# Eight matmuls of a shared network moved from ahead of the first slot table to behind the third

## The reference, cut to what matters

```
scores = softmax(flat_x @ gate_w.T).T
topk_weight, topk_idx = top_k(scores, C)          # C = 148 tokens for each of 16 experts
xg = flat_x[topk_idx]
h  = gelu(xg @ Wg.T) * (xg @ Wu.T)                 # per expert, 1024 wide
eo = (h @ Wd.T) * topk_weight
out = scatter_add(eo) + (gelu(x @ Sg.T) * (x @ Su.T)) @ Sd.T   # shared network, 512 wide
```

## Time and profile before

| | |
|---|---|
| runs shown | 535.07, 536.86, 537.45 us |
| median | 536.86 us |
| profiled execution | 538.24 us, span 536.4 us |
| TensorE matmul | 470.9 us busy (88%) |
| VectorE | 395.4 us (74%) |
| ScalarE | 228.5 us (43%) |
| GpSimd | 192.2 us (36%) |
| mean granted clock of TensorE | 0.957 |
| HBM read, written | 63.32 MB, 5.33 MB |

### The profile page before, as it was taken

How to read it: one execution, slowest core, us unless ns; L and a number is a source line. 1 busy time by engine, 2 the same in 40 slices (tenths; PEclk the granted TensorE clock), 3 DMA queues, 4 the chain that set the end, 5 groups by cost and what they waited for, 6 DMA issues and landing times.

```text
span 536.4 us, 10728 instructions
## 1 busy us (share of the span) xinstructions
PE 470.9 (88%) x3873; PEld 409.7 (76%) x3873; DVE 395.4 (74%) x694; ACT 228.5 (43%) x529; POOL 192.2 (36%) x252
## 2 busy tenths in 40 slices
PE   6968989889898986969998886999999999999990
PEld 3546867759577683959786675889999999999990
DVE  1398998989989898696227969768866777667730
ACT  1413463544545446121334300455556665566610
POOL 1313245363543634040210005128444453454242
PEclk9989999999999999788987999899999999999996
DMA  7855110100000000000000000697888898899521
GB/s 243 334 201 222 34 41 1 42 10 31 23 18 10 10 0 10 1 10 1 10 11 6 1 2 21 214 384 265 282 292 315 319 324 294 298 331 328 174 26 12
DMA packets 17344, 69.05 MB, mean 129 GB/s; under 512 B 4338, under 2 KB 10399, under 8 KB 12834
## 3 DMA queue, kind: packets, MB, share of 16 engines
q1 hardware_dynamic: 12130, 61.96, 31.0%
q0 software_dynamic: 4608, 5.41, 4.9%
q10 hardware_dynamic: 576, 1.29, 0.7%
HBM read 63.32 MB, written 5.33 MB: 128 GB/s over the span
## 4 chain that ended last, share of the span: by engine, by line
PE 62%; DVE 13%; POOL 6%; ACT 6%; issue 5%; DMA 3%; DVEq 0%; POOLq 0%; SPq 0%; ACTq 0%
PE bank L1446 16%; PE bank L1457 11%; PE bank L1231 7%; PE bank L1204 7%; PE bank L1217 6%; POOL tmp L423 3%; PE bank L1355 3%; PE bank L1243 3%; DMA wex_s<-in_wex 2%; DVE scratch L994 2%; PE bank L1158 2%; DVE wproj_s L977 2%; ACT L539 2%; PE bank L1193 1%; POOL rstd L425 1%
## 5 line engine op out<-in xcount | busy, mean ns | idle before, releaser
L423 POOL TENSOR_SCALAR tmp<-mv 128x1 f32<-128x1 f32 x30 | 34.0, 1134 | 164.7 <-DVE mv L792 164.7
L507 POOL DMA_INDIRECT out_rows<-scratch,slot_s x32 | 52.1, 1629 | 85.4 <-DMA out_rows<-scratch,slot_s 66.0
L1457 PE MATMUL bank<-scratch,wex_s 128*128 128x148 f32 x512 | 77.7, 295 | 0.5 <-DVE scratch L1086 0.5
L1457 PEld LDWEIGHTS bank<-scratch,wex_s 128*128 128x128 f32 x512 | 67.6, 190 | 1.0 <-DVE scratch L1086 1.0
L496 POOL DMA_INDIRECT xg<-token_rows,slot_g x32 | 40.1, 1253 | 75.2 <-issue 59.8
L736 ACT ACTIVATE scratch<-bank 128x296 f32<-128x296 f32 x64 | 26.6, 416 | 69.5 <-PE bank L1446 69.5
L1446 PE MATMUL bank<-scratch,wfc_s 128*128 128x148 f16 x512 | 52.8, 228 | 0.8 <-DVE wproj_s L977 0.8
L1446 PE MATMUL bank<-scratch,wsh_s 128*128 128x148 f16 x512 | 52.7, 227 | 0.0
L1446 PE MATMUL bank<-scratch,wproj_s 128*128 128x148 f16 x256 | 50.7, 227 | 0.0
L1086 DVE SCALAR_TENSOR_TENSOR scratch<-bank,scratch 128x296 f32<-128x296 f32 x64 | 29.5, 461 | 27.1 <-ACT scratch L736 26.9
L977 DVE SCALAR_TENSOR_TENSOR wproj_s<-wex_s,wfc_s 128x512 f16<-128x512 f32 x64 | 40.4, 683 | 11.2 <-ACT wfc_s L719 11.2
(11 more groups left out here) (164 smaller groups left out, 943.6 us busy)
## 6 DMA issues: line engine op xcount, KB each, us to landing
wex_s<-in_wex SPq DMA_DIRECT2D x16, 2048.0 KB
wex_s<-in_wex SPq DMA_DIRECT2D x16, 1024.0 KB, 8.5
patch_s<-in_patches SPq DMA_DIRECT2D x10, 384.0 KB
token_rows<-y_s SPq DMA_DIRECT2D x10, 128.0 KB, 1.7
out_rows<-h_all SPq DMA_DIRECT2D x5, 256.0 KB
wfc_s<-in_wfc SPq DMA_DIRECT2D x1, 1024.0 KB, 5.1
wproj_s<-in_wproj SPq DMA_DIRECT2D x1, 1024.0 KB, 7.3
wsh_s<-in_wsh SPq DMA_DIRECT2D x1, 1024.0 KB, 9.0
```

The lines of the kernel that those rows point to most:

```text
L423: gp.tensor_scalar(tmp[:, k:k + 1], var, EPS, None, ALU.add).then_inc(p_chain, 1)
L507: gp.indirect_dma_start(out, bass.IndirectOffsetOnAxis(slot_s[b][:], 0), eo[b], None, compute_op=ALU.add).then_inc(scattered, 16)
L1457: last = pe.matmul(ps_down[k][:, 0:C], wex_s[s.par][:, lo:lo + P], hexT[:, m, :], start=(m == 0), stop=(m == MC - 1))
```

## The change

After the thresholds are found and the prefix sums made, 30 matmuls of the shared network's down projection remain. Before, 18 of them stand ahead of the first slot table, 4 behind it, 4 behind the second, none behind the third, and 4 behind the transposes of the first expert's rows. After, 10 stand ahead of the first table and 8 behind the third one. Their order among themselves is the same.

```diff
             left = STEPS + 4 * TILES - BEFORE - sum(BESIDE)
-            assert left >= 12
-            fill(left - 12)
+            assert left >= 20
+            fill(left - 20)
             pe.wait_ge(digits_made, 1)
             slots(0)
             fill(4)
             slots(1)
             fill(4)
             slots(2)
+            fill(8)
```

## The result

| | before | after |
|---|---|---|
| runs | 6: 535.05 to 537.45 us | 6: 532.09 to 533.78 us |
| median | 536.50 us | 532.83 us |
| profiled execution, span | 538.24, 536.4 us | 532.39, 530.6 us |
| mean granted clock | 0.957 | 0.969 |

The changed kernel is faster: ratio 0.9937, 95% interval 0.9916 to 0.9958, that is 3.4 us (2.3 to 4.5). Values from 0.9943 to 0.9958, that is 2.3 to 3.1 us, fit both measurements. Three of the 64 runs of the kernel before in the later comparisons took 695 to 1650 us and are left out of the ratios.

What follows compares the result with a forecast made beforehand. TensorE was taken as the bound, VectorE leading from 325.4 to 335.0 us. 0.9 us from the earlier table and 2.2 from the clock made 3.1 off 538.24, giving 535.1; the median lies 1.4 lower, so 533.8, range 532.4 to 537.0.

Steps and rivals of the forecast that it cites:

- (a): Ahead of the first slot table: with eight matmuls fewer, VectorE takes that table 0.9 us earlier.
- (b): VectorE's run from first to third table: keeps its 9.46 us, as each piece still finds its input.
- (c): Behind the third table: the moved matmuls' 3.50 us fit in the 3.79 us stall, costing nothing at full clock.
- (d): Transposes to first expert's products: full clock kept, products 3.1 us earlier together with (a), 2.2 of it the clock's.
- (e): Downstream, third expert's weights: the last shared tile releases their queue earlier too, so idle time stays; term 0.
- Rival 1: Gap ahead of the first table: the clock falls there instead; gain 0.9 us (536.0) or 2.6 (534.3); chance 0.15.
- rival 2: From the gap ahead of the first table: the clock falls and does not recover; slower, 539.2 us; chance 0.08.
- Rival 3: Expert stage: third expert's weights set the pace and the lead is lost; 536.0 us; chance 0.15 together with Rival 4.
- Rival 4: Only (a) is gained, the clock falling elsewhere ahead of the experts; 535.9 us; chance 0.15 together with Rival 3.
- rival 2's full case: The extreme of rival 2, the clock falling ahead of the first table without recovering: 540.5 us.
- The rule weighed: TensorE's clock: avoid idle gaps above about 3 us; the new 1.9 us gap would be harmless, giving 533.8 us.

Runs made afterwards that it cites:

- e3: The change with twelve matmuls moved behind the third slot table instead of eight; ratio to the kernel before 1.0034.
- e1: The kernel before with 16 unused matmuls between the third slot table and the wait ahead of the transposes, nothing moved; ratio 0.9967.
- e6: The change with 14 unused matmuls (3.0 us) between the last shared tile and the first expert; ratio to the kernel before 0.9957.
- e7: The change with SyncE waiting for two pairs of the first expert's products before issuing the second expert's down weights; ratio to the kernel before 1.0023.
- e11: The changed kernel itself, measured and profiled again beside three others; ratio to the kernel before 0.9957.
- e4: The change with the eight matmuls put behind the transposes of the first expert's rows instead of ahead of them; ratio to the kernel before 1.0064.
- e8: The change with SyncE issuing the third expert's gate and up weights ahead of its wait for the shared tiles; ratio to the kernel before 0.9900.
- e10: e8 with five unused matmuls ahead of the first search round; ratio to the kernel before 0.9884.
- e9: The kernel before with SyncE issuing the third expert's gate and up weights ahead of its wait for the shared tiles; ratio 0.9950.
- e2: The change with four matmuls moved behind the third slot table instead of eight; ratio to the kernel before 0.9953.

## Why the prediction was right, and where it was not

The time came out at 532.83, forecast 533.8, range 532.4 to 537.0; forecast 3.1 us less, measured 3.4 and, again, 2.3. The first products of the third expert are 2.5 us earlier; the profiles do not show where the rest of the 3.4 comes from.

(a) **Right.** VectorE takes the first table 0.99 us earlier (forecast 0.9), and TensorE waits 1.80 us for the one-hot (forecast 1.9).

(b) **Right.** VectorE's run is 9.44 us long (forecast 9.46). None of the sums came late, though two tiles fewer are done at the first table.

(c) **Right.** The moved eight fit, and 0.23 us of waiting are left (forecast 0.3). e3 shows the bound: with four more TensorE is the late one.

(d) **Right in its size, not in its path.** The first products are 2.99 us earlier (forecast 3.1), and e1 shows 2.0 of them to be the clock's (forecast 2.2). But the low half of the rows, which was to be late next, was done 1.74 us after the transposes' start (333.27, forecast 2.02), and the products began at 2.25 us, when the four matmuls behind the transposes ended (333.86 in the chain).

(e) **Wrong in its mechanism, nearly right in its number.** What TensorE starts earlier "comes out at the end, if the weights come earlier too", the prediction says. The condition was named, and it held in the change, but the two stand the wrong way round: the weights set the pace and TensorE's start is the condition. e6 started TensorE 3.0 us later and lost 0.35; e7 held back the weights and lost 4.0. The idle time of 1.2 us from 355 to 365 was read as a small remainder. It was the sign that the weights come late. The full measure of it is the whole stretch from A to C: 24.4 us where 22.2 would do. The chain of waits had said so, with the landing on it. The number came out since the same event, the last shared tile, releases both TensorE and SyncE's queue, as the step said; with an edit that moves only one of the two it would not have. The term was put at 0; it lost 0.5 us. The transfer took 0.4 us longer (12.61 against 12.23), and 12.77 in e11. Why is open. One guess is the next expert's weights, which were issued 5.8 us behind these in the change and 6.5 before, and so ran beside them for longer; but in e7 they were issued 2.5 us behind, and the transfer took 12.34.

Rival 1 was real, and cheaper than priced. The clock did not fall in the new gap in six profiled executions that have it (the change, e11, e4, e6, e7, e8). In e10, with the same order of the tables, it fell right behind the gap, at about 321.8, and stayed at half for about 3.4 us. The prediction put such a stretch at 0.5 us over the slack; A is 16.91 there as in the change, so the slack covered it. Its longer form, rival 2, did not occur with eight moved and did with twelve. Rival 3 was right on who sets the pace and wrong on the result. Rival 4 is refuted by A and by e1. The 540.5 us of rival 2's full case stands there without a working, and no run here shows it.

The rule weighed: the Trainium skill, page "TensorE: Matmul & The Clock Gate", section "Why this matters for your kernels", warns of idle gaps above about 3 us. The traces agree in that the clock fell in the stalls of 3.79 us and was kept in most gaps of 1.8 us, but they differ from it as a limit: the clock fell behind the gap of 2.3 us in the search and, in e10 alone of seven executions, behind that of 1.8 us with a table of narrow matmuls after it. It fell 1.1 us into the stall of 3.79 us in e9, 1.6 us into the same stall in the kernel before and 2.6 us into it in e4. So the outcome differs from one execution to the next at one length of the gap. Whether what stands behind a gap matters (e2 kept the clock over 1.96 us between dense stretches, in its one profile) was not tested.

Of the 5.8 us between the two spans, 2.5 lie ahead of the digits and 2.5 between the digits and C. The last 0.8 lie within the experts, between the low halves of the rows (L983) of the fifth and the eighth: 35.24 us before, 34.41 in the change and 34.37 to 34.52 in all the others. The one profile of before stands alone with it; its cause is open.

## What to carry to other kernels

A stall in which TensorE waits for another engine was paid for twice here: 3.8 us of waiting, and 2.0 us of half clock behind it (e1). Independent work that is due anyway belongs there, and not ahead of the step that another engine waits for. Take no more than the stall holds: four or eight matmuls moved gave 2.3 us or more, twelve lost 1.8. When an edit moves one event, list all that this event releases. Here the DMA queue behind it mattered more than the matmuls, and the cheapest gain (2.6 us more) was to issue a ready transfer ahead of a wait that it does not need.

## What was not expected of the hardware

The start of the digits differs by up to 2.5 us between executions, with the same code ahead of it; the granted clock of earlier stretches differs along with it. Most medians here lie within 0.5 us of what the distances behind it give. At half clock, once fallen, TensorE stayed 10 us in e3 although it was busy for 9.1 of them, broken by the narrow matmuls of the tables, and 3.4 us in e10. A table of twenty narrow matmuls took 1.40 us at half (e3) and 0.85 at full: even with 4 columns per matmul, each behind a load of 74 columns of weights, the clock is felt. And a delayed transfer cost more than its delay: in e7 it made TensorE wait 4.1 us by way of two other engines, and the clock fell in that wait.
